# An accumulating DMA in place of a GpSimd addition for the attention's bias row

## What is computed

```python
h = layernorm(x) * (1 + ca) + sa
qkv = h @ Wqkv + bqkv                      # q, k, v of 256 columns
attn = softmax(q @ k.T / 16)
x = x + ga * (attn @ v @ Wo + bo)
h = layernorm(x) * (1 + cb) + sb
x = x + gb * (h @ weight.T + bias + lora)  # lora: two products of rank 16 for some batches
```

## Time and profile before

| | us |
|---|---|
| median of 3 runs (1152.84 to 1154.0) | 1152.91 |
| the profiled execution | 1153.4 |
| its span in the profile | 1151.6 |
| TensorE busy in it | 1084.6 |
| VectorE busy | 632.7 |
| ScalarE busy | 381.0 |
| GpSimd busy | 241.9 |

### The profile page before, as it was taken

How to read it: one execution, slowest core, us unless ns; L and a number is a source line. 1 busy time by engine, 2 the same in 40 slices (tenths; PEclk the granted TensorE clock), 3 DMA queues, 4 the chain that set the end, 5 groups by cost and what they waited for, 6 DMA issues and landing times.

```text
span 1151.6 us, 13779 instructions
## 1 busy us (share of the span) xinstructions
PE 1084.6 (94%) x5593; PEld 895.4 (78%) x5593; DVE 632.7 (55%) x837; ACT 381.0 (33%) x630; POOL 241.9 (21%) x211
## 2 busy tenths in 40 slices
PE   7799998999999999989999997999989999999996
PEld 2576997888987889878889875788777877787775
DVE  1830256463455462565625658737767776677631
ACT  0831144241343231542315443403422332323310
POOL 1000011231111221021401233233134122324122
PEclk9799999999998999999999998999999999999998
DMA  9975201533014340124310678543525462454221
GB/s 326 374 271 198 77 1 47 194 124 112 1 37 147 115 178 1 38 92 164 135 48 19 178 276 290 183 164 110 202 80 194 145 202 75 163 201 164 97 86 55
DMA packets 51968, 160.26 MB, mean 139 GB/s; under 512 B 5217, under 2 KB 9729, under 8 KB 51905
## 3 DMA queue, kind: packets, MB, share of 16 engines
q1 hardware_dynamic: 42208, 125.01, 31.4%
q0 software_dynamic: 9696, 34.36, 7.9%
HBM read 121.60 MB, written 37.75 MB: 138 GB/s over the span
## 4 chain that ended last, share of the span: by engine, by line
PE 64%; DVE 12%; issue 9%; DMA 6%; ACT 5%; POOL 3%; SPq 0%; DVEq 0%; POOLq 0%; ACTq 0%
PE pairA L1106 5%; PE pairB L1106 5%; PE pairA L1107 5%; PE pairC L1106 5%; PE pairA L1108 5%; PE pairB L1108 5%; PE pairB L1107 5%; PE pairC L1108 5%; PE pairC L1107 5%; PE pairD L1106 4%; PE pairD L1108 4%; PE pairD L1107 4%; ACT xs L770 2%; DVE w_sum L1065 2%; DVE bn L957 2%
## 5 line engine op out<-in xcount | busy, mean ns | idle before, releaser
L986 DVE TENSOR_TENSOR h_lo<-xs,h_hi 128x512 fp32r<-128x512 f32 x120 | 84.0, 741 | 91.3 <-ACT h_hi L778 91.0
L682 POOL TENSOR_TENSOR rstd<-mv,eps 128x2 f32<-128x2 f32 x32 | 9.1, 285 | 584.2 <-DVE mv L962 584.2
L957 DVE BATCH_NORM_STATS2 bn<-xs 128x6 f32<-128x512 f32 x120 | 75.3, 681 | 38.5 <-DMA xs<-x_dram 19.5
L1106 PE MATMUL pairA<-w_hi,h_hi 128*128 128x512 f32 x208 | 83.2, 400 | 11.2 <-issue 7.6
L978 DVE TENSOR_SCALAR xs<-xs,mv,rstd 128x1024 f32<-128x1024 f32 x60 | 82.7, 1420 | 18.6 <-POOL rstd L684 18.6
L703 POOL TENSOR_TENSOR res<-res,row_bc 128x1024 f32<-128x1024 f32 x32 | 80.1, 2518 | 24.4 <-ACT row_bc L734 14.5
L690 POOL TENSOR_TENSOR xr<-xr,row_bc 128x1024 f32<-128x1024 f32 x32 | 77.2, 2414 | 27.3 <-DMA xr<-in_L_attn_x 27.0
L848 ACT ACTIVATE w_hi<-w_sum 128x1024 fp32r<-128x1024 f32 x32 | 34.0, 1061 | 147.1 <-DVE w_sum L1065 147.0
L1107 PE MATMUL pairA<-w_lo,h_hi 128*128 128x512 f32 x208 | 82.0, 394 | 0.0
L1108 PE MATMUL pairA<-w_hi,h_lo 128*128 128x512 f32 x208 | 81.8, 393 | 0.0
L1106 PE MATMUL pairB<-w_hi,h_hi 128*128 128x512 f32 (+1 forms) x192 | 72.3, 376 | 0.0
(11 more groups left out here) (313 smaller groups left out, 2622.4 us busy)
## 6 DMA issues: line engine op xcount, KB each, us to landing
wm<-in_L_wmod SPq DMA_DIRECT2D x48, 512.0 KB, 7.0
xr<-in_L_attn_x SPq DMA_DIRECT2D x32, 512.0 KB, 3.6
x_dram<-xr POOLq DMA_DIRECT2D x32, 512.0 KB, 3.1
xs<-x_dram SPq DMA_DIRECT2D x32, 512.0 KB, 4.3
w2t<-w2t_dram SPq DMA_DIRECT2D x32, 512.0 KB, 4.5
res<-x_dram SPq DMA_DIRECT2D x32, 512.0 KB, 5.2
out_y<-res POOLq DMA_DIRECT2D x32, 512.0 KB, 3.4
xs<-in_L_attn_x SPq DMA_DIRECT2D x28, 512.0 KB, 5.0
```

The costliest lines, as they stand in the source:

```text
L957: nc.vector.bn_stats(bn[:, k, half, :], rows[:, k, half * BANK:(half + 1) * BANK]).then_inc(bn_made, 1)
L986: nc.vector.tensor_tensor(lo, h, hi.bitcast(F32), ALU.subtract).then_inc(h_lo_made, 1)
L1106: nc.tensor.matmul(out, left[0], right[0], start=first, stop=False)
```

## The change

The 32 GpSimd additions of the first half become 32 DMAs from GpSimd's queue, each of which adds the 128 x 1024 numbers of `row_bc` onto the same tile of `xr`, in place. They have a semaphore per buffer, as each adds 16 to it on completion. L1044 waits for the one of its buffer, and ScalarE's copy into `row_bc` for both. The order of the steps, the additions of the second half (L703) and all loads and stores are as before.

```diff
-        residual_made = sem("residual_made")
+        residual_made = [sem(f"residual_made{i}") for i in range(2)]
...
                     pool.wait_ge(ld_xr[t % 2], 16 * (QT // 2 * b + t // 2 + 1))
                     pool.wait_ge(row_made, b + 1)
                     xt = xr[:, t % 2, :]
-                    nc.gpsimd.tensor_tensor(xt, xt, row_bc[:, :], ALU.add).then_inc(residual_made, 1)
+                    pool.dma_start(xt, row_bc[:, :], accum_op=ALU.add).then_inc(residual_made[t % 2], 16)
...
                     act.wait_ge(row_done, b + 2)
-                    wait(act, residual_made, QT * (b + 1))
+                    for k in range(2):
+                        wait(act, residual_made[k], 16 * (QT // 2) * (b + 1))
                     emptied_copy(row_bc[:, :], ps[:, :], row_made)
...
                     dve.wait_ge(o_done, QT * b + t + 1)
-                    dve.wait_ge(residual_made, QT * b + t + 1)
+                    dve.wait_ge(residual_made[t % 2], 16 * (QT // 2 * b + t // 2 + 1))
                     dve.wait_ge(r_total_made, QT * b + t + 1)
```

## The result

The changed kernel takes 1179.8 us (median of four runs, 1175.8 to 1183.0) against 1152.9 for the kernel before: a ratio of 1.023, 95% interval 1.0197 to 1.0262. The forecast of 1158 had the sign right and a fifth of the size, and its range ended at 1174.

The account below looks back on a forecast made before the run. TensorE, busy 94% of the span, was taken to bound the kernel. Batches 0 to 2 lose 6.1 us, the last gains 0.7: 5.4 added to the profiled 1153.4, less 0.5, gives 1158 us, range 1147 to 1174.

Parts of the forecast that it names:

- What bounds the kernel: Whole kernel: TensorE is busy 94% of the span; L690 costs by blocking VectorE's normalisations and by delaying L1044's bias.
- part 1: Removing 32 GpSimd adds: normalisations fall from 3.60 to 1.53 us, 2.07 us gained in each of batches 0 to 2.
- Part 2: The 32 accumulating transfers: each takes 4.9 us from issue to semaphore, 5.5 behind a store, against 2.4 for GpSimd's add.
- Part 3: Later bias in batches 0 to 2: TensorE waits 3.7 us at tile 5, 0.4 at tile 3, nothing at tile 7.
- the sum: Whole kernel: 6.1 us lost in batches 0 to 2 less 0.7 gained in the last batch, 5.4 us more.
- Last batch: [...] Gained: 0.7: Last batch, tiles 6 and 7: L1044 of tile 6 starts 0.5 us earlier, that of tile 7 0.7 earlier; 0.7 gained.
- The DMA engines I take to have room: Whole kernel: the load of the DMA engines was set to zero in the forecast.
- the clock at zero: TensorE's clock: old waits shrink, a new 3.7 us one comes per batch; one slow stretch is 3 us either way, counted zero.
- Much slower: All transfers: add at a third of a copy's rate or worse, or issue as long as GpSimd's add; 1173 us, 17%.
- Faster: All transfers: about as quick as a copy, 3.1 us, 3.7 behind a store; 1143 us, 25% with values up to 4.0.
- no difference: All transfers: 4.0 to 4.6 us each, so gain and loss cancel to within 2.3 us, 0.2%; 13%.
- The blocked issue: Tile 5's issue: VectorE's normalisations hold up GpSimd's descriptor writing by up to 0.8 us, three times; 1160 us, 5%.

## Why the forecast was wrong

**What bounds the kernel, and part 1** held. The collision of L690 with the normalisations was real, and worth 1.8 us a batch where 2.07 stood. Undone by itself it gives 0.9% or 10 us, more than three times 1.8; the stretch of low clock that goes with the waits, some 2.7 us of batch 1, is part of the difference, the rest stays open. One reading in it was wrong: "tiles 3, 4 and 7 of each batch wait directly for the bias" is true of batches 0 to 2, nine of the ten L1044. The tenth is tile 5 of the last batch, see below.

**Part 2, the transfer's price**, held where the DMA engines are idle: 4.64 us for 4.9, 5.6 behind a store for 5.5. In the packet records an adding packet of 4 KB takes 341 ns and a copied one 162. The rule of the Trainium skill that stands in part 2 (Collectives: The Full Stack, "The bandwidth ceiling") is borne out as to the rate: 2.1 times as long a packet. The two descriptors themselves no record shows; an adding transfer counts as many packets and bytes as a store or a copy. What puts the clean transfer above its 4.3 fits the dearer issue, 0.90 us against 0.57 for a store: half of the 0.6 us that the forecast gave it.

**Part 3, batches 0 to 2**, held: waits behind tile 5 of 3.6 to 3.9 us (3.7), before the pairB transposes 0.3 to 1.1 (0.4), nothing behind tile 7. From the waits: 11.1 + 1.8 lost, 3.6 + 1.2 gained, 8.1 us for the 6.1 of the sum. The rest of the 11.4, 3.3 us, fits the clock: 13.6 us at the lower level in these batches against 6.8.

**The step that failed first is "Last batch: [...] Gained: 0.7".** It took the transfer at 4.9 and 5.5 us in the stretch with the most other transfers, on the sentence "The DMA engines I take to have room". No row stood behind it: the window of the last batch had a DMA share of 0.60, and 0.94 from 699 to 708. There the transfers take 5 to 11 us. And it reckoned tiles 6 and 7 only. Tile 5 waited directly for the bias in the last batch, and TensorE for tile 5, in the kernel before:

```profile
696.80 2.35 POOL L690 TENSOR_TENSOR xr<-xr,row_bc 128x1024 f32<-128x1024 f32 x1 [5.41 <-DMA xr<-in_L_attn_x]
...
699.25 1.28 DVE L1044 SCALAR_TENSOR_TENSOR xr<-pairC,r_total,xr 128x1024 f32<-128x1024 f32 x1 [2.42 <-issue]
...
700.59 0.89 PE L1236 MATMUL pairC<-b_stack,pick_b 128*128 128x512 f32 x2 [2.53 <-DVE xr L1044]
```

With the forecast's own 4.9 us that L1044 would have started at 701.7, 2.4 us late (my estimate), and TensorE with it, so the forecast lacked this term even for idle DMA engines. Measured, TensorE's waits for the output tile grew from 5.5 us (2.5 + 2.0 + 1.0) to 14.5 (6.0 + 4.7 + 2.3 + 1.5), and the batch by 10.2; tile 6, which was to come 0.5 us earlier, made TensorE wait 4.7. The run with DMA in this batch alone (+1.45%) shows that its transfers bring the loss. That the load of the DMA engines is the reason is shown for tiles 6 and 7 by the lighter loads, and likely for tile 5; for tiles 2 and 4 no run tests it.

**The second step that failed is the clock at zero**, with "one stretch more or less is 3 us either way". In the attention of before TensorE had the lower level (1.2 of 2.4 GHz) for 17 us: at 346, 701 and 721. Now it has it for 34: at 256, 413, 567, 707, 717, 731 and 744. At half speed 17 us more are 8.5 us of work lost if TensorE is busy throughout; its busy time says 7.5. The window around the one at 567, behind batch 2's tile 5, and the same window of the kernel before:

```profile
566.00:573.00 7.00, 5.58 (x13) 4.43 (x14) 3.69 (x5) 2.85 (x6) 1.43 (x2) 0.55 0.75 198
```

```profile
566.00:573.00 7.00, 7.00 (x56) 6.78 (x55) 4.01 (x4) 1.76 (x2) 3.45 (x3) 1.00 0.39 153
```

56 matmul records against 13 in the same 7 us. Each of the three new stretches of batches 0 to 2 begins within 1.5 us of the end of a wait behind tile 5. The forecast named that wait as new and then let the one stretch it took away stand for the three it brings. What a stretch costs can be read from batches 0 to 2 where they are those of the kernel before, in four profiles: 151.7 to 152.0 us without one, 153.3 to 153.7 with one of 3.4 us, 154.5 with one of 6.8. No run tests the clock alone: that waits start the stretches is read from where they lie. In the five profiles with waits of 3.5 to 4.2 us behind tile 5 of batches 0 to 2, all 15 have a stretch that begins within 2 us of their end; with tile 5 alone, waits of 1.4 to 1.6 us, none of the three has, and with tile 4 alone, 1.5 to 2.0 us before its transposes, two of three have. The shorter waits are not as regular: the kernel before has the same 1.2 + 1.7 us in batches 0, 1 and 2, and in this profile a stretch in batch 1 alone. Why some last 3.4 us and some 6.8 or more stays open.

**The rivals.** "Much slower" came out nearest by its number, 1173, and by the wrong mechanism: the add runs at half a copy's rate, not at a third, and the issue holds GpSimd for 0.90 us, not for the add's 2.4. "Faster" and "no difference" fall with 4.64 us, and the run with copies bears their reasoning out for batches 0 to 2 only: at a copy's speed the kernel takes 1154, not 1143, because of the last batch. The blocked issue falls as a cause of the loss, as tile 5's issue took its 0.90 us, but an issue does suffer. Beside the normalisations it took 1.01 us in batches 0 to 2 and 1.27 at 723.72, elsewhere mostly 0.84 to 0.91; a copy's went from 0.54 to 1.01. So the warning of the Trainium skill (SBUF — State Buffer, "SBUF: two separate sides") fits these traces, at 0.1 to 0.5 us a time, while the exclusion of GpSimd's add and the normalisations, which the same section describes, is worth 2 us a time.

## What to carry to other kernels

Price a transfer at the load of the stretch in which it falls, not at its median over the kernel: the same 512 KB took 4.6 us with the DMA engines otherwise idle and 5 to 11 us in the last batch. Go through the tiles of a batch with another order of steps anew: what waits for what was different there. A wait of 3 to 4 us that is new can cost more than itself (8.1 us of waits went with 11.4 us of time in batches 0 to 2), so give each such wait a term for the clock. And where two engines exclude each other, try first to move the instruction: one addition moved 20 steps up a list gave 0.9%, what the replacement was worth at its best.

## What the runs showed of the hardware that I had not expected

- An adding DMA from SBUF to SBUF is dearer at every stage than a copy: issue 0.90 us against 0.55, a 4 KB packet 341 ns against 162, landing at best 4.6 us against 2.9.
- Its neighbours land later: the loads of `xr` after a median of 4.4 and 4.5 us in the two profiles in place of 3.6, where the copies left 3.6. For the stores (3.5 and 3.2 in place of 3.1) this isn't clear.
- In two executions of the same program the same transfer took 5.1 us when it was issued 3 us before two row loads and 10.0 us when it was issued beside them.
- An adding transfer's issue on GpSimd took 1.01 us beside VectorE's normalisations in batches 0 to 2, a copy's too, in place of 0.90 and 0.54.
